# An attention and mixture-of-experts kernel on one core: first loads reordered, the router's second half moved ahead of the key norms, and the final sums shared by VectorE and TensorE

## What is computed

```python
mod = (silu(c) @ wmod).reshape(8, 6, 1, 256)          # sa, ca, ga, sb, cb, gb
ga, gb = (sign * maximum(abs, 0.25) of each)
h = layernorm(x) * (1 + ca) + sa
x = x + ga * attn(h)
h = layernorm(x) * (1 + cb) + sb
x = x + gb * ffn(h)
```

## Time and profile before

| | us |
|---|---|
| median of 3 runs | 464.38 (462.05 to 474.47) |
| the profiled execution, device time | 467.52 |
| its span, first to last instruction | 465.8 |
| VectorE, TensorE, GpSimd, ScalarE busy | 282.6, 285.5, 213.3, 96.7 |
| granted TensorE clock, mean | 0.76 of full speed |

### The profile page before, as it was taken

How to read it: one execution, slowest core, us unless ns; L and a number is a source line. 1 busy time by engine, 2 the same in 40 slices (tenths; PEclk the granted TensorE clock), 3 DMA queues, 4 the chain that set the end, 5 groups by cost and what they waited for, 6 DMA issues and landing times.

```text
span 465.8 us, 7039 instructions
## 1 busy us (share of the span) xinstructions
PE 285.5 (61%) x2286; PEld 209.3 (45%) x2286; DVE 282.6 (61%) x1061; ACT 96.7 (21%) x253; POOL 213.3 (46%) x311
## 2 busy tenths in 40 slices
PE   2468795958949769699497645100799999900000
PEld 2454584846838648577386433000455544400000
DVE  0845425596594776955937596600577755429994
ACT  3231220413303215032032100000144323300000
POOL 2401102111754656647644648777055545426664
PEclk9569587995986979859879785655699995655555
DMA  7630799999933214004031000000889971069981
GB/s 254 187 135 2 166 383 339 268 292 247 339 118 123 84 50 146 9 34 143 32 109 42 2 5 5 2 4 3 294 248 285 280 186 34 16 234 367 327 309 45
DMA packets 63464, 71.60 MB, mean 154 GB/s; under 512 B 8021, under 2 KB 58849, under 8 KB 63430
## 3 DMA queue, kind: packets, MB, share of 16 engines
q1 hardware_dynamic: 43270, 51.31, 37.8%
q10 hardware_dynamic: 14016, 15.21, 9.3%
q0 software_dynamic: 6144, 4.66, 3.4%
HBM read 46.29 MB, written 40.93 MB: 187 GB/s over the span
## 4 chain that ended last, share of the span: by engine, by line
PE 31%; issue 18%; DVE 17%; POOL 16%; DMA 12%; ACT 3%; DVEq 1%; SPq 0%; POOLq 0%; ACTq 0%
POOL rows_dram L431 8%; PE ps_s L1320 4%; DMA y_dram<-osq,y_rows 4%; PE ps_o L1214 4%; PE ps_a L1119 3%; DMA egu<-y_dram 3%; DVE z L1041 3%; DVE scm L841 3%; PE ps_c L1241 3%; PE ps_b L1232 2%; POOL h2s L441 2%; POOL h2row L445 2%; DMA pre<-in_L_attn_x 2%; PE ps_o L1210 2%; PE ps_a L1222 2%
## 5 line engine op out<-in xcount | busy, mean ns | idle before, releaser
L431 POOL DMA_INDIRECT rows_dram<-h2row,slot_ix x96 | 95.4, 994 | 51.6 <-issue 18.2
L415 POOL TENSOR_TENSOR rstd<-ve,half_exp 128x2 f32<-128x2 f32 x15 | 11.2, 750 | 96.3 <-DVE ve L673 96.3
L1041 DVE TENSOR_REDUCE z<-egu 128x256 f32<-128x1536 f32 x16 | 42.8, 2750 | 10.9 <-DMA egu<-y_dram 10.9
L419 POOL TENSOR_TENSOR pool_pad<-half_exp 128x1 f32<-128x1 f32 x72 | 13.9, 193 | 55.7 <-ACT oT L552 19.8
L841 DVE TENSOR_TENSOR scm<-ps_s,decay 128x2048 f32<-128x2048 f32 x16 | 36.5, 2282 | 4.2 <-PE ps_s L1193 4.2
L1214 PE MATMUL ps_o<-scm,v_eo 128*32 128x128 f32 x512 | 26.8, 357 | 11.8 <-DVE scm L841 11.8
L1320 PE MATMUL ps_s<-egu,x 128*64 128x192 f32 x256 | 32.8, 383 | 0.1
L1222 PE MATMUL ps_a<-ident,h2row 128*128 128x128 f32 x32 | 8.9, 434 | 36.5 <-POOL h2row L445 36.5
L552 ACT ACTIVATE h2T<-ps_a 128x512 f32<-128x512 f32 x8 | 4.8, 598 | 107.4 <-PE ps_a L1222 107.4
L1006 DVE COPY x<-ps_a 128x256 f32<-128x256 f32 x16 | 6.7, 419 | 31.4 <-PE ps_a L1309 31.4
L1214 PEld LDWEIGHTS ps_o<-scm,v_eo 128*32 128x32 f32 x512 | 16.9, 138 | 17.1 <-issue 16.3
(11 more groups left out here) (219 smaller groups left out, 723.5 us busy)
## 6 DMA issues: line engine op xcount, KB each, us to landing
y_dram<-y_zeros ACTq DMA_DIRECT2D x8, 1536.0 KB, 6.8
egu<-y_dram SPq DMA_DIRECT2D x16, 768.0 KB, 5.4
egu<-in_L_ffn_w_gate SPq DMA_DIRECT2D x16, 384.0 KB, 8.5
egu<-in_L_ffn_w_up SPq DMA_DIRECT2D x16, 384.0 KB, 9.0
ed<-in_L_ffn_w_down SPq DMA_DIRECT2D x16, 384.0 KB, 11.3
rows_dram<-y_zeros SPq DMA_DIRECT2D x1, 5376.0 KB, 28.6
mod_b<-mod_dram SPq DMA_DIRECT2D x8, 384.0 KB, 3.7
pre<-in_L_attn_x SPq DMA_DIRECT2D x8, 256.0 KB, 4.2
```

The source lines that it names most:

```text
L419: return g.tensor_tensor(pool_pad[:, at:at + 1], half_exp[:, 0, 0:1], half_exp[:, 0, 0:1], ALU.add)
L431: g.indirect_dma_start(out=rows_dram, out_offset=bass.IndirectOffsetOnAxis(ap=slot_ix[b % HBUF][:, tile, j:j + 1], axis=0), in_=h2row[b % ...
L1041: v.tensor_reduce(ysum[m % NT], y_in[m].rearrange("p (j c) -> p c j", c=C), AX_X, ALU.add).then_inc(S["y_sum"], 1)
```

## The change

There are four groups of edits in one kernel.

1. **First loads.** ScalarE's queue loads the query, key and value weights alone. wmod and the projection weights move to SyncE's queue and are issued once image 0 has landed; the shared weights and images 1 to 7 follow, the latter without the wait for the sum of absolute values.
2. **Prologue order.** VectorE sums the absolute values ahead of the c columns. GpSimd's first square root moves behind its constants, and its select on the decay mask waits for both ternary weights (q_w at 2). hsq is made from hT in one instruction (any step), and TensorE waits for it only at the statistics.
3. **Steps.** `router_choice(s-2)` stands in front of `rms(s)`.
4. **Final sums.** A buffer holds two tiles (an image). VectorE adds rows 3 to 5 onto rows 0 to 2 (128 x 1536), TensorE adds the three by six matmuls with the identity into one of two PSUM banks, VectorE multiplies by gb and adds `pre` for an image at a time, and ScalarE's queue stores 256 KB. GpSimd has no part, and the loops are written out. All loads are still on SyncE's queue.

```diff
@@ sync
             load_x(0)
+            wmod_v = wmod.rearrange("(k p) n -> p k n", p=P)
+            sp.wait_ge(S["ld_x0"], 16)
+            sp.dma_start(wmod_sb[:, :, 0:2 * C], wmod_v[:, :, 0:2 * C]).then_inc(S["ld_wmod"], 16)
+            sp.dma_start(proj_raw, proj_w.rearrange("(a p) c -> p a c", p=P)).then_inc(S["ld_projw"], 16)
+            sp.dma_start(wmod_sb[:, :, 2 * C:6 * C], wmod_v[:, :, 2 * C:6 * C]).then_inc(S["ld_wmod_gates"], 16)
...
-            load_x(1)
-            sp.wait_ge(S["q_abs"], 1)
-            for b in range(2, B):
+            for b in range(1, B):
                 load_x(b)
...
-            for t in range(YBUF):
-                load_y(t, t)
-            with sp.Fori(0, B * NT // YBUF - 1) as i:
-                for m in range(YBUF):
-                    sp.wait_ge(S["y_sum"], YBUF * i + (m + 1))
-                    load_y(YBUF * i + (m + YBUF), m)
-                    store_out(YBUF * i + m, m % NT)
...
+            def load_y(b):
+                for i in range(NT):
+                    sp.dma_start(y_in[b % YBUF][:, i].rearrange("p j c -> p (j c)"), y_v[NT * b + i]
+                                 ).then_inc(S[f"ld_y{b % YBUF}"], 16)
+
+            for b in range(YBUF):
+                load_y(b)
+            for b in range(YBUF, B):
+                sp.wait_ge(S["y_sum"], b - YBUF + 1)
+                load_y(b)
@@ gpsimd
+            pool.wait_ge(S["ln1_ve"], 1)
+            g.tensor_tensor(rstd1[:], ve1[:], half_exp[:, 0], ALU.pow).then_inc(S["ln1_rstd"], 1)
+
             pool.wait_ge(S["c_decay0"], 1)
+            pool.wait_ge(S["q_w"], 2)
@@ scalar
-                for j in range(KC):
-                    last = a.activation(hsq[:, j], ps_a[:, N * j:N * j + N], ACT.Square,
-                                        scale=mod_cols[:, 2 + j, b:b + 1], bias=mod_cols[:, j, b:b + 1])
-                last.then_inc(S["hsq_ready"], 1)
+                act.wait_ge(S["hT_ready"], b + 1)
+                a.activation(hsq[:], hT[:], ACT.Square).then_inc(S["hsq_ready"], 1)
...
+            for b in range(B):
+                act.wait_ge(S["y_out"], b + 1)
+                a.dma_start(out_t[b], pre[:, NT * b:NT * b + NT]).then_inc(S["st_out"], 16)
@@ vector
+                if has_two:
+                    router_choice(s - 2)
                 if cur:
                     rms(s, par)
-                if has_two:
-                    router_choice(s - 2)
...
+            def half_sums(b):
+
+                y = y_in[b % YBUF]
+                dve.wait_ge(S[f"ld_y{b % YBUF}"], 16 * NT * (b // YBUF + 1))
+                v.tensor_tensor(y[:, :, 0:3], y[:, :, 0:3], y[:, :, 3:6], ALU.add).then_inc(S["y_half"], 1)
+
+            half_sums(0)
+            for b in range(B):
+                if b + 1 < B:
+                    half_sums(b + 1)
+                dve.wait_ge(S["y_sum"], b + 1)
+                v.tensor_tensor(ygb[b % 2][:], ysum[b % 2][:].rearrange("p (i c) -> p i c", i=NT),
+                                spread(gb_all[:, b], 1, NT), ALU.mult).then_inc(S["y_gb"], 1)
+                dve.wait_ge(S["y_gb"], b + 1)
+                v.tensor_tensor(pre[:, NT * b:NT * b + NT], ygb[b % 2][:], pre[:, NT * b:NT * b + NT],
+                                ALU.add).then_inc(S["y_out"], 1)
@@ tensor, project_qkv: the wait on hsq_ready goes from the query matmuls to the statistics
+            for b in range(B):
+                y = y_in[b % YBUF]
+                pe.wait_ge(S["y_half"], b + 1)
+                seen(pe, S["y_gb"], b - 1)
+                for i in range(NT):
+                    for j in range(3):
+                        last = mm.matmul(ysum[b % 2][:, C * i:C * i + C], ident[:], y[:, i, j], start=(j == 0), stop=(j == 2))
+                last.then_inc(S["y_sum"], 1)
```

More of the change, by code:

```diff
@@ L210, in adaln_attention_moe @@
         abs_rows, sign_rows = h2s[0:B], z2[0:B]
-        y_in = [flat[:, TOPK * C * i:TOPK * C * (i + 1)] for i in range(YBUF)]
-        ysum = [z1[:, i] for i in range(2)]
-        ygb = [h2s[:, i] for i in range(2)]
-        yout = [z2[:, i] for i in range(2)]
+        y_in = [flat[:, NT * TOPK * C * i:NT * TOPK * C * (i + 1)].rearrange("p (i j c) -> p i j c", i=NT, j=TOPK)
+                for i in range(YBUF)]
+        ygb = [z1, qT]
         ps_s = ctx.enter_context(nc.psum_tensor("ps_s", [P, 4, 512], F32))
@@ L246, in adaln_attention_moe @@
         x_t = x.rearrange("b (i p) c -> b p i c", p=P)
-        out_t = out.rearrange("b (i p) c -> (b i) p c", p=P)
+        out_t = out.rearrange("b (i p) c -> b p i c", p=P)
         wg_v = w_gate.rearrange("(r e) (p k) f -> r p e k f", e=4, k=KC)
@@ L518, in _ @@
                 put(q, q % OBUF, q % WBUF, 16 * ((q + 1) // OBUF) if q >= OBUF - 1 else None)
-            def gate(t, b, i):
-                pool.wait_ge(S["y_sum"], t + 1)
-                pool.wait_ge(S["settled"], 2 * t + 1)
-                settle(4).then_inc(S["settled"], 1)
-                g.tensor_tensor(ygb[i], ysum[i], gb_all[:, b], ALU.mult).then_inc(S["y_gb"], 1)
-                pool.wait_ge(S["y_gb"], t + (NT + 1))
-                pool.wait_ge(S[f"st_y{i}"], 16 * b + 16)
-                pool.wait_ge(S["settled"], 2 * t + 2)
-                settle(4).then_inc(S["settled"], 1)
-                g.tensor_tensor(yout[i], ygb[i], pre[:, t], ALU.add).then_inc(S["y_out"], 1)
-            for i in range(NT):
-                pool.sem_inc(S[f"st_y{i}"], 16)
-            pool.sem_inc(S["settled"], 1)
-            pool.sem_inc(S["y_gb"], NT)
-            with pool.Fori(0, B) as b:
-                for i in range(NT):
-                    gate(NT * b + i, b, i)
         @block.scalar
@@ L545, in _ @@
             a.dma_start(qkv_raw, qkv_w.rearrange("(a p) c -> p a c", p=P)).then_inc(S["ld_qkvw"], 16)
-            wmod_v = wmod.rearrange("(k p) n -> p k n", p=P)
-            a.dma_start(wmod_sb[:, :, 0:2 * C], wmod_v[:, :, 0:2 * C]).then_inc(S["ld_wmod"], 16)
-            a.dma_start(proj_raw, proj_w.rearrange("(a p) c -> p a c", p=P)).then_inc(S["ld_projw"], 16)
-            a.dma_start(wmod_sb[:, :, 2 * C:6 * C], wmod_v[:, :, 2 * C:6 * C]).then_inc(S["ld_wmod_gates"], 16)
             def copy(out_, in_, scale=1.0):
@@ L691, in _ @@
             norm1_stats(0)
+            dve.wait_ge(S["ld_qkvw"], 16)
+            v.tensor_reduce(abs_sum[:, 0:1], qkv_raw, mybir.AxisListType.XY, ALU.add,
+                            apply_absolute_value=True).then_inc(S["q_abs"], 1)
             cn_t = ps_o[:, 0:KC * (B + 3)].rearrange("p (k n) -> p k n", k=KC)
@@ L1034, in _ @@
             pair_steps(pair_step)
-            with dve.Fori(0, B * NT // YBUF) as i:
-                for m in range(YBUF):
-                    dve.wait_ge(S[f"ld_y{m}"], 16 * i + 16)
-                    dve.wait_ge(S["y_gb"], YBUF * i + (m + 1))
-                    v.tensor_reduce(ysum[m % NT], y_in[m].rearrange("p (j c) -> p c j", c=C), AX_X,
-                                    ALU.add).then_inc(S["y_sum"], 1)
+            def half_sums(b):
[12 more added lines that the diff above has]
+                                ALU.add).then_inc(S["y_out"], 1)
         @block.tensor
```

26 lines of the change are left out of this document (8 added, 18 removed).

## The result

The changed kernel takes **441.42 us** (median of 4, 438.75 to 449.54), the kernel before in the same comparison 464.02 (4, 462.05 to 474.47): ratio 0.950, 95% interval 0.944 to 0.956. The prediction was 448 (441 to 457): the direction is right, the time is 6.6 us shorter than forecast. Some runs of these kernels are 1.5% and more longer than the fastest of the same kernel; ratios and intervals leave those out, the medians in us hold them.

| stretch | before | after | gained | forecast |
|---|---|---|---|---|
| first query matmuls start | 28.05 | 18.99 | 9.1 | 6.4 |
| from there to the load of the experts' rows | 298.2 | 296.3 | 1.9 | 7.5 |
| from there to the first final load (experts) | 85.4 | 79.5 | 5.9 | 0 |
| from there to the end (final sums) | 54.1 | 44.7 | 9.4 | 2.5 |

What follows compares the result with a forecast made beforehand. No engine leads throughout: an engine-to-engine chain bounds the steps, transfers the changed final stage. Gains 6.4 + 7.5 + 2.5 = 16.4 us take the profiled 467.5 to 451.1; the median being 3.1 lower, 448 us, range 441 to 457.

Steps and rivals of the forecast that it cites:

- Prologue: Work ahead of step 0: 6.0 + 0.9 - 0.5 = 6.4 us gained, ends 3.8 and 8.9.
- Image 0: Prologue: image 0 lands at 6.8 instead of 12.8, gaining 6.0 us.
- the wait for wmod: Prologue: VectorE waits 0 to 1.6 us for wmod before the modulation columns; 0.5 taken as cost.
- the select: Prologue: GpSimd's mask select still holds a decay-sum instruction, gain 0; if it holds none, 2.0 us more.
- Steps: Router ahead of rms: four times 1.7 and twice 1.1 us, less 1.5 for GpSimd: 7.5 us, ends 2.8 and 9.0.
- The rival of the modulation row: Steps: modulation rows of images 2 and 3 land around 122, later steps lose 1 to 3 us: 450; chance 0.06.
- Final sums: Final stage: last load at 452, end at 463.3 for 465.8, so 2.5 us gained, ends -0.3 and 7.8.
- So the transfers bound it: Final stage: transfers, not VectorE or TensorE, set the time; 370 GB/s taken, 38.2 us, last load at 452.
- The chain behind the last landing: Final stage, after the last load: 1.75 + 2.5 + 0.7 + 0.7 + 0.4 of waits = 6.05 us.
- six matmuls against eight rows: Final stage: TensorE's six adding matmuls take 2.5 us per image, from eight of 256 columns taking 3.38 us in step 0.
- the transfers run at the loads' rate: Rival, final stage: transfers keep the loads-alone rate, 433 GB/s, to the end: 448 - 5.3 = 443; chance 0.12.
- The clock rival: Steps: TensorE's clock stays halved up to L1158, six steps lose 8 us each: 496, slower; chance 0.04.

Runs made afterwards that it cites:

- first pair of traces: The first profiled executions of the kernel before and of the changed kernel: 467.52 and 441.21 us.
- the second trace: Profile of the changed kernel run again without edits; that run measured 437.91 us, ratio 0.948 to the kernel before.
- with the row early: Changed kernel with image 2's modulation rows loaded between the fourth and fifth of nine expert-weight groups, not behind the ninth: 430.91 us, 0.932 to the kernel before.
- the kernel before with half sums: Kernel before with its final reductions over three of the six rows of a token, half the additions left out: 460.94 us, ratio 0.993.
- where VectorE was slowed: Changed kernel with one more unused 2048-column reduction on VectorE ahead of each image's half sum: 450.61 us, ratio 0.964 to the kernel before.

## Why the prediction was short, step by step

The step that failed is the rate in the final stage; it is the third point. The other two parts came out at the forecast numbers, partly by luck.

- **Prologue: 6.4 forecast, 6.4 measured alone** (2.9 to 10.0 by the interval). Its parts are off and the interval hides it. The first query starts 9.1 us earlier. Image 0 gives 6.3 us for the 6.0; the wait for wmod costs 0 for 0.5; and the select holds nothing, which gains 2.0 for 0. The prediction named that last case and its price, and chose the other. The GPSIMD Engine Reference of the Trainium skill (Key points) says that GpSimd contends with VectorE instructions in a 2-port mode or with two SBUF inputs. The three instructions of the decay sums beside the select have one input each and took 0.14 to 0.16 us, the one held for 1.97 us in the earlier trace rows has two: both agree. But a fourth one, L719, has two inputs as well. It runs just ahead of the select, by 0.15 to 0.16 us in every profiled execution with the new prologue, so the 2.0 us hang on that order too and not on the rule alone.
- **Steps: 7.5 forecast, 7.5 alone, 5 to 6 in the whole, 1.9 in the first pair of traces.** The mechanism held: the state waits for L1142 again (by 0.67 us in step 3 of the second trace). The number did so by luck: the 7.5 us of the move alone hold a wait of 4.9 us for the modulation row, and with the row early the move is worth about 10, or 2.2 us a step where 31.3 to 29.8 was forecast. The rival of the modulation row was given 0.06 and 1 to 3 us; it came true with 3.9 and 6.0 us. It had the landing right (122 for 122.79) and the use too late: 121.5, where the state is done at 118.9. The late semaphore belongs to the execution; the second trace, without it, is 1.4 us shorter in that stretch.
- **Final sums: 2.5 forecast, 9.4. This is the step that failed**: "So the transfers bound it", at 370 GB/s, read from a DMA share of 0.98 at 347. Full engines were taken for engines at their rate. The transfers do bound the stage, but after moves 403 GB/s where before moves 343; counted as the prediction counted, from 2.3 us behind the first issue, it is some 420 (13.9 MB in 33.1 us) for the 370. The last half sum starts 35.9 us after the first issue where the prediction's 452 - 411.7 is 40.3: 4.4 of the missing 6.9 us. The chain behind the last landing has the right length, 6.1 us from 430.74 to 436.87 for 6.05, by two errors that cancel. The prediction set six matmuls against eight rows, but those eight rows are four matmuls, and the six are twelve rows. And it took the halved clock. At that clock an image takes 5.46 us (402.87), not 2.5; the last one takes 2.86 because the granted clock is 1.00 by then, after TensorE has been adding since 402.87. The other 2.6 us are at the very end: 2.6 us from the last addition to the end, where 4.9 + 0.3 was carried over from before. Of that, the span goes on 3.5 us behind the last packet in every kernel with the old final stage, whatever its depth, and 0.8 in every kernel with the new one, with stores on either queue. What those 2.7 us are was not tried.
- The rival "the transfers run at the loads' rate" (0.12, 443 us) is what happened, and not by the mechanism it named. A mix of loads and stores does not slow them: after moves 416 GB/s with loads alone and 404 to 422 with both. A shallow loop does. What the prediction drew from DMA: Bandwidth & Descriptors (Issuing engines are not separate DMA queues) of the Trainium skill, that the stores' queue is worth nothing, agrees with 44.4 us on one queue and 44.7 on two.
- The clock rival did not come: over 195 us of the steps the granted clock was 0.85 where the earlier trace rows has 0.84.

## What to carry to other kernels

A DMA share near 1.0 says that packets are under way, not that they go at their speed: set the rate against the best rate of the same packets elsewhere in the trace, and look at how many transfers are in flight, before calling it a ceiling. When steps get shorter, follow each transfer that isn't behind them in the queue but behind other transfers: its time does not move, and it turns from hidden to a wait at one step. (With the router's move alone the row is issued at 117.59 us, for 117.72 before, and is needed 5 us sooner than it lands.) And time a stage in more than one profiled execution before explaining it: two of the four differences in the first table were of the execution, in part or in full.

## What the runs showed of the hardware

- The time of one packet goes with how deep its loop is loaded: 6144 bytes take 234 ns by the median in all kernels, but 138 to 205 of 2048 take over 350 ns with four tiles in flight, and 15 to 45 with eight (82 where VectorE was slowed), over all twenty traces.
- The semaphore that a group of 32-row matmuls raises can come up to 2.7 us late. It did so in steps 3 to 7, where GpSimd sends rows beside the scores, in the first trace of after and in all four kernels that ran on one chip one after the other, the kernel before with half sums among them (1.04, 1.40, 2.69, 1.21, 0.60 us). In fourteen executions profiled on four other chips, and in that of before, it was 0.04 to 0.06 us everywhere, with the same code and the same transfers beside it. The same code had it in one execution and not in another, so it does not go with the kernel; chip and time of the run are not parted; what it is stays open. Where VectorE has other work in front of the mask, it costs nothing.
- The experts' stage took 77 to 80 us in twelve executions and 81 to 88 in eight, at a mean granted clock of 0.91 to 0.94 in the first and 0.81 to 0.90 in the second, with the same code.
